# Moving products and weighings from VectorE to GpSimd, and a scaling to ScalarE, in a four-layer kernel on one core

## The chip, the core and the metric

The kernel runs on one core of a Trainium2 chip. Its engines are TensorE (PE in the profile, its weight loads PEld), VectorE (DVE), ScalarE (ACT), GpSimd (POOL) and SyncE (SP), which only issues DMAs here. The metric is the device time of one execution in microseconds; lower is better.

## What is computed

One sequence of 1024 tokens of width 256 passes through four blocks, each followed by a layer norm of the input plus the block's output:

```python
x = layernorm(x + selective_scan_block(x))   # layer 0: 32 states, 256 channels
x = layernorm(x + quantized_ffn(x))          # 704 hidden
x = layernorm(x + mamba_block(x))            # layer 1: conv, 16 states, 512 channels, gate
x = layernorm(x + attention_and_experts(x))  # 16 heads of 128; 16 experts, 6 a token, and a shared one
```

Both scans have the same core, for each channel d and state n:

```python
delta = softplus(projection + bias)
h[t] = exp(delta[t] * A[d, n]) * h[t-1] + (delta[t] * u[t]) * B[t, n]
y[t] = sum_n h[t] * C[t, n]
```

In layer 0 u is the input itself, in layer 1 the convolved and activated input. The attention is causal, behind a root-mean-square norm (`x * rsqrt(mean(x^2) + eps) * w`); a second such norm stands ahead of the experts, where each expert's hidden value `silu(g) * up` is multiplied by the token's weight for this expert and projected down.

## The kernel before

The tokens are taken in four chunks of 256 (c = 0 to 3). A scan unit is one state n of a pair of channel tiles (2 x 128 channels by 256 tokens); each layer has 32 units a chunk, 256 units in all. For a unit:
- SP fetches the state's B and C rows, broadcast to all partitions (`bc_rows`, five buffers, L1303).
- ScalarE makes the decays exp(delta * A), two instructions, into a PSUM bank (L1700).
- GpSimd makes the drive: `w` times the B row (L2291), w being delta times u.
- VectorE scans, two instructions of 128x256 (L1957), and multiplies the states by the C row (L1969; in chunk 0 GpSimd does so for a quarter of the units, L2301).
- ScalarE copies the last states into `h_end` for the next chunk (L1713).
- In chunk 0 TensorE adds the units up in PSUM (L1410), in the others GpSimd does (L2321).

Between the scans of layer 0 and layer 1 of a chunk lies a chain of small steps (norms, the quantized FFN, the convolution, projections, softplus). Softplus ends in `softplus_sum` on VectorE: four elementwise instructions on 128x512, then delta (L2020), then w, by L2028 in layer 0 and by L2024 in layer 1, where the factor 0.5 is part of it. There are three softplus calls a chunk (layer 0, and two halves of layer 1), so 12 in all. `x_proj` (L1483) makes the time step and the B and C rows of layer 1 from the weight `w_x1`, which ScalarE halves once (`chore`, L1682).

Behind layer 1 a chunk goes through the attention, 16 heads one after the other, which VectorE and ScalarE share (maxima L2144, exponentials L1865, moves L2160 and L1876). Ahead of the heads (r = 0) and ahead of the experts (r = 1) stands the root-mean-square norm: ScalarE squares with a row sum (L1813), VectorE takes the mean (L2129), GpSimd the power -1/2 (L2324), VectorE scales the tokens into `hn` (`rms_scale`, L2135, two instructions), TensorE turns them (L1394), ScalarE moves them into `hT` (L1826).

The experts run in 13 groups of up to two tiles: 2 shared and 11 routed. For a group TensorE makes gate and up (L1388), ScalarE a tanh (L1907), VectorE two products (L2240, L2248) and for the 11 routed groups the weighing by `cw_rows`, the routing weights of 128x512 (`weigh_up`, L2259); TensorE projects down (L1652). Four `hh` buffers hold the groups.

The order of instructions on each engine is not written by hand. A planner (`weave`, L738) holds lanes of stages; each stage has parts with an engine and an assumed cost, events it comes after, events it gives, and a lag behind its end. Again and again it takes, over all lanes, the part with the smallest key:

```python
start = max(ready, clock[engine])
key = (start - lane.bonus * EARLIER[engine], -lane.bonus, ready)
```

and emits it, if it belongs to the engine being written. So the costs and each lane's bonus set the order in every queue, the DMA queue of SP included. Twelve weight loads (L1289) have a lane of their own: load i comes after scan i + 1.

Of the kernel before, what the change touches and what calls it, by code (L numbers as in the profile page):

```python
# [17 lines left out]
P = 128  # L18
# [30 lines left out]
AOTS, HIDDENS = 3, 4  # L49

# [46 lines left out]
def blocks(c):  # L97

    return SIZES[c] // P
# [64 lines left out]
class Idle:  # L164
# [7 lines left out]
    load = load_x = dbc = project_dt = softplus_abs = softplus_x = softplus_log = softplus_sum = chore = nothing  # L172
# [55 lines left out]
DMA = "sp", 0.3  # L228
# [34 lines left out]
class Units:  # L263
# [20 lines left out]
    def fetches(self):  # L284
        total = CHUNKS * sum(UNITS)
        while len(self.order) < total:
# [12 lines left out]
            yield Stage(partial(self.p.fetch, g, c, layer, k), (DMA,), after, (("rows", g),), lag=3.0)  # L299
# [23 lines left out]
    def drives(self):  # L323
        for unit in self.each():
# [4 lines left out]
            after = [("delta", c, 0 if layer == 0 else 1 + k // STATE1), ("rows", g)]  # L329
# [78 lines left out]
class Chain:  # L408
# [6 lines left out]
    def lanes(self):  # L415
        return [Lane(self.first(), 0.20, 8), Lane(self.second(), 1.30, 16)]

    def softplus(self, c, g, given, use):
# [8 lines left out]
        before = (("decays", b, layer), ("drives", b, layer)) if b >= 0 else ()  # L427
        yield Stage(partial(p.softplus_sum, c, g), (dve(size, *[2 * size] * 5),),
                    (("log", c, g), ("x", c, g), *before), (("delta", c, g), ("scratch", "softplus", c, g)))

    def first(self):
        p = self.p
        for c in range(CHUNKS):
            size = SIZES[c]
            yield Stage(partial(p.load_x, c), (DMA,), (("y", c - 2, 0),) if c > 1 else (), (("x0", c),), lag=4.0)
# [70 lines left out]
    def second(self):  # L506
        for c in range(CHUNKS):
# [6 lines left out]
         "ident_b", "w_o")  # L514
FFN_LOADS, MAMBA_LOADS = 3, 7
# [14 lines left out]
class Attention:  # L530
# [5 lines left out]
    def lanes(self):  # L536
        return [Lane(self.into_heads(), 0.60, 8), Lane(self.projections(), 0.60, 8), Lane(self.scores(), 1.00, 6),
                Lane(self.products(), 1.10, 8), Lane(self.results(), 1.10, 8), Lane(self.experts(), 2.50, 2),
                Lane(self.routing(), 1.50, 8), Lane(self.weights(), 2.20, 2),
                Lane(self.hidden(), 1.20, 6),  # L540
                Lane(self.weighed(), 1.90, 4), Lane(self.sums(), 1.80, 6)]

    def rms(self, c, r, given):
# [7 lines left out]
        yield Stage(partial(p.rms_scale, c, r), (dve(*[DIM + 150] * n),), (("rms", c, r),), (("scaled", c, r),))  # L551
# [3 lines left out]
    def into_heads(self):  # L555

        p = self.p
        for c in range(CHUNKS):
            for h in range(HEADS):
# [6 lines left out]
                yield Stage(partial(p.fetch_head, c, h), (DMA,), after, (("head_w", c, h),), lag=4.0)  # L566
                if c:
                    yield Stage(partial(p.place, c, h), (DMA,), self.kv_free(c, h), (("past", c, h),), lag=4.0)

# [86 lines left out]
    def experts(self):  # L656

        p = self.p
        for c in range(CHUNKS):
            for n in range(len(FETCHES)):  # L660
# [9 lines left out]
                yield Stage(partial(p.fetch_expert, c, n), (DMA,), after, (("expert", c, n),), lag=4.5)  # L670
# [15 lines left out]
    def weights(self):  # L686

        p = self.p
        for c in range(CHUNKS):
            for r, rows in enumerate(CW_ROWS):  # L690
                bc, br = divmod(c * ROUTED_GROUPS + r - CW, ROUTED_GROUPS)
                free = (("weighted", bc, SHARED_GROUPS + br),) if bc >= 0 else ()
                yield Stage(partial(p.fetch_weights, c, r), (("sp", 0.1 * len(rows)),), (("cwT", c), *free),
                            (("cw", c, r),), lag=4.0)
# [13 lines left out]
    def weighed(self):  # L708
        p = self.p
        for c in range(CHUNKS):  # L710
            for g in range(SHARED_GROUPS, N_GROUPS):
                width = len(GROUPS[g]) * SIZES[c]
                yield Stage(partial(p.weigh_up, c, g), (dve(width),),
                            (("cw", c, g - SHARED_GROUPS), ("raised", c, g)), (("weighted", c, g),))

    def sums(self):
        p = self.p
        for c in range(CHUNKS):
# [8 lines left out]
            yield Stage(partial(p.store, c), (DMA,), (("out", c),), (("hn", c, 2),), lag=4.0)  # L727

EARLIER = {'pe': 0.2, 'dve': 0.2, 'act': 0.7, 'pool': 1.0, 'sp': 1.0}


LOADED = {("first",): 5.5}
# [1708 lines left out]
```

## Time and profile before

| | |
|---|---|
| median of 3 runs | 1362.71 us (1359.16 to 1363.14) |
| profiled execution | 1363.67 us, of which the span of instructions is 1362.4 |
| mean granted TensorE clock | 0.922 |
| busy: TensorE, its weight loads | 1119.7 us (82%), 879.8 us (65%) |
| busy: VectorE, ScalarE, GpSimd | 1030.9 us (76%), 596.2 us (44%), 600.4 us (44%) |
| DMA | 191.54 MB, mean 141 GB/s |

Shares are of the span. The durations below come from the one profiled execution. A line number can be that of a helper: L1388 is every projection on TensorE.

### The profile page before, as it was taken

To read this page: it belongs to the slowest core of one execution; us is meant where nothing else is said; L and a number is where in the kernel's file an instruction comes from. 1 tells how busy PE (TensorE), PEld (TensorE's weight loads), DVE (VectorE), ACT (ScalarE), POOL (GpSimd) and SP (SyncE) were. 2 spreads that over 40 slices of the span, in tenths; PEclk is the share of its full clock that TensorE was granted. 3 is DMA by queue.
4 is the path that set the end of the run, shared out by engine and by line. 5 is a ranking of instruction groups with operands and counts; after the bars stand their busy time and mean duration, and the time that the engine had idled before them with its cause. 6 is when DMAs were issued, how large, how long until landed. Compare 5 with 4: busy or idle time off the path is not lost. (4 is left out here: it accounts for less than half of the span.)

```text
span 1362.4 us, 17002 instructions
## 1 busy us (share of the span) xinstructions
PE 1119.7 (82%) x5224; PEld 879.8 (65%) x5224; DVE 1030.9 (76%) x1879; ACT 596.2 (44%) x1543; POOL 600.4 (44%) x487
## 2 busy tenths in 40 slices
PE   4557536499695899977977899799998999999797
PEld 2335324377584678755855787587877877777586
DVE  5797899989999999999997885699944444444433
ACT  4553555454664336555753232565532123333210
POOL 3577477964575687654875640176600000000000
PEclk9798758899797999998988999899999999999899
DMA  4652124353254775433765641266543643222173
GB/s 135 251 195 74 48 88 142 108 158 105 85 174 155 218 232 166 136 101 111 210 216 156 196 144 43 83 201 199 162 144 104 204 136 104 95 93 81 58 210 103
DMA packets 105434, 191.54 MB, mean 141 GB/s; under 512 B 11648, under 2 KB 42368, under 8 KB 105088
## 3 DMA queue, kind: packets, MB, share of 16 engines
q1 hardware_dynamic: 91520, 177.42, 41.9%
q10 hardware_dynamic: 13824, 13.05, 3.1%
q8 instruction: 41, 0.67, 0.2%
q14 instruction: 49, 0.40, 0.1%
HBM read 176.33 MB, written 14.09 MB: 140 GB/s over the span
## 5 line engine op out<-in xcount | busy, mean ns | idle before, releaser
L1957 DVE TENSOR_TENSOR_SCAN scan_banks<-scan_banks,h_end,drive 128x256 f32<-128x256 f32 x480 | 338.5, 742 | 13.9 <-POOL drive L2291 11.0
L2321 POOL TENSOR_TENSOR sum<-sum,state 128x512 f32<-128x512 f32 x174 | 227.3, 1306 | 54.4 <-DVE state L1969 52.3
L2291 POOL TENSOR_TENSOR drive<-w0T,bc_rows 128x512 f32<-128x512 f32 x128 | 164.3, 1291 | 152.0 <-DVE scan_banks L1957 98.0
L2291 POOL TENSOR_TENSOR drive<-w1T,bc_rows 128x512 f32<-128x512 f32 x128 | 163.4, 1283 | 139.6 <-DVE scan_banks L1957 61.4
L2324 POOL TENSOR_TENSOR stats_b<-stats_b,neg_half 128x2 f32<-128x2 f32 x12 | 8.8, 732 | 367.4 <-DVE stats_b L2129 200.8
L1969 DVE TENSOR_TENSOR state<-scan_banks,bc_rows 128x512 f32<-128x512 f32 x240 | 162.7, 678 | 0.6
L1410 PE MATMUL score_banks<-state,ident 128*128 128x256 f32 x256 | 85.2, 483 | 79.3 <-DVE state L1969 44.7
L1560 PE MATMUL score_banks<-kv,qT 128*128 128x512 f32 (+3 forms) x360 | 135.7, 493 | 6.4 <-ACT probs L1865 3.7
L2144 DVE TENSOR_REDUCE soft<-score_banks 128x1 f32<-128x128 f32 (+4 forms) x122 | 88.0, 729 | 61.9 <-PE score_banks L1562 61.6
L1865 ACT ACTIVATE probs<-score_banks,soft 128x128 f32<-128x128 f32 (+4 forms) x122 | 87.8, 721 | 97.5 <-DVE soft L2144 96.7
L1410 PEld LDWEIGHTS score_banks<-state,ident 128*128 128x128 f32 x256 | 57.2, 239 | 107.5 <-DVE state L1969 57.4
L1585 PE MATMUL work_bank<-probsT,kv 128*128 128x256 f32 x504 | 120.6, 363 | 5.3 <-DVE pad_hs L2107 2.7
L1388 PE MATMUL work_bank<-hT,streamed_w 128*128 128x256 f32 x496 | 122.0, 388 | 1.5 <-ACT kv L1834 1.4
L1700 ACT ACTIVATE scan_banks<-delta1T,a 128x256 f32<-128x256 f32 x256 | 111.4, 470 | 24.6 <-DVE state L1969 17.1
L1700 ACT ACTIVATE scan_banks<-delta0T,a 128x256 f32<-128x256 f32 x256 | 110.9, 468 | 25.3 <-DVE state L1969 22.0
L1388 PEld LDWEIGHTS work_bank<-hT,streamed_w 128*128 128x128 f32 x496 | 92.3, 195 | 14.2 <-ACT kv L1834 2.2
L1585 PEld LDWEIGHTS work_bank<-probsT,kv 128*128 128x128 f32 x504 | 87.9, 193 | 15.2 <-DVE probsT L2160 3.6
L1713 ACT ACTIVATE h_end<-scan_banks 128x2 f32<-128x2 f32 x176 | 29.7, 171 | 154.5 <-DVE state L1969 138.4
L1560 PEld LDWEIGHTS score_banks<-kv,qT 128*128 128x128 f32 x360 | 63.4, 194 | 42.4 <-issue 33.8
L1394 PE MATMUL work_bank<-ident,probs 128*128 128x128 f32 x450 | 72.7, 280 | 16.8 <-DVE pad_hs L2107 7.5
L2160 DVE COPY probsT<-work_bank 128x512 f32<-128x512 f32 (+2 forms) x132 | 58.6, 471 | 23.5 <-PE work_bank L1394 22.9
L1394 PEld LDWEIGHTS work_bank<-ident,probs 128*128 128x128 f32 x450 | 53.2, 144 | 35.8 <-issue 9.8
(203 smaller groups left out, 2098.6 us busy)
## 6 DMA issues: line engine op xcount, KB each, us to landing
bc_rows<-bc_rows SPq DMA_DIRECT2D x256, 256.0 KB, 3.8
streamed_w<-in_w_head SPq DMA_DIRECT2D x64, 384.0 KB, 5.0
expert_w<-in_w_moe SPq DMA_DIRECT2D x52, 384.0 KB, 4.4
kv_past<-kv ACTq DMA_DIRECT2D x48, 256.0 KB, 3.2
kv<-in_w_moe SPq DMA_DIRECT2D x32, 384.0 KB, 3.9
kv<-kv_past SPq DMA_DIRECT2D x16, 768.0 KB, 4.7
kv<-kv_past SPq DMA_DIRECT2D x16, 512.0 KB, 5.0
streamed_w<-in_w_moe SPq DMA_DIRECT2D x16, 384.0 KB, 4.1
```

The source lines that it names most:

```text
L1388: instruction = self.matmul(to, weight, m, start=k == 0, stop=k == len(weights) - 1)
L1394: instruction = self.transpose(b[:, at:at + P], src, ident[:, :])
L1410: done = self.matmul(to[:, i, :], ident[:, :], tiles[:, i, :], start=n == 0 and i == 0, stop=n == STATES[layer] - 1, skip_group_check=True)
L1560: self.matmul(to[:, at:upto], q[h % 2][:, qb * P:(qb + 1) * P], tile[:, 0, at:upto], start=True, stop=upto < n_keys)
L1585: mm = self.matmul(b[:, lo:hi], tile[:, 1, kb * HEAD:(kb + 1) * HEAD], moving[:, i * hi + lo:(i + 1) * hi], start=kb == 0, stop=kb == last ...
L1700: done = self.activation(to[:, i * size:(i + 1) * size], delta_of(layer, c)[:, kt, 0:size], ACT.Exp, scale=a_rate[layer][:, kt, n:n + 1])
L1865: self.activation(probs[probs_at(c, h, qb)][:, 0:n_keys], b[:, 0:n_keys], ACT.Exp, bias=st[:, 0, qb:qb + 1], accum_out=st[:, 1, qb:qb + 1] ...
L1957: done = e.engine.tensor_tensor_scan(states, decays, drive[g % len(drive)][:, i, 0:size], h_end[layer][:, n, kt:kt + 1], ALU.mult, ALU.add)
L1969: self.tt(slot_of(c, layer, k), by_tile(unit_bank(g, size), size), rows_of(g, c, 1), ALU.mult).then_inc(weighed, 1)
L2144: e.engine.tensor_reduce(st[:, 0, qb:qb + 1], b[:, 0:keys(c, qb)], AX.X, ALU.max, negate=True).then_inc(neg_max, 1)
L2291: self.tt(drive[g % len(drive)][:, :, 0:size], w_of(layer, c)[:, PAIR * half:PAIR * (half + 1), 0:size], rows_of(g, c, 0), ALU.mult).then_ ...
L2321: self.tt(to, so_far, slot_of(c, layer, k), ALU.add).then_inc(added, 1)
```

## The change

- **Products.** `softplus_sum` on VectorE ends with delta. A new stage `delta_x` on GpSimd multiplies delta by the input (x0 or hs) into w. The factor 0.5 of layer 1 goes into the B columns of `w_x1`: the one ScalarE instruction on this weight becomes three, with 0.5, 0.25 and 0.5. delta's last add waits for the previous product that used the buffer, not for the drives; the drives are waited for by `delta_x`.
- **Scaling.** `rms_scale` moves from VectorE to ScalarE, a Copy with a scale for each token.
- **Weighing.** `weigh_up` of chunks 0 and 1 moves from VectorE to GpSimd; chunks 2 and 3 stay.
- **Loads.** Load i comes after scan 2i + 1.
- **Planner.** New costs for matmuls, turns and DMAs (these now by size, as time of the SP queue), new lags, and a new bonus for 20 lanes and new factors on it by engine (`EARLIER`).

```diff
+WEIGHED_BY_POOL = 2
 def pe(*columns):
-    return "pe", sum(0.018 + 0.00172 * n for n in columns)
+    return "pe", sum(0.012 + 0.00169 * n for n in columns)
 def pe_turn(n):
-    return "pe", 0.13 * n
+    return "pe", 0.115 * n
-DMA = "sp", 0.3
+def dma(kilobytes):
+    return "sp", max(0.5, kilobytes / 230)
...
-        return [Lane(self.fetches(), 0.00, 1), Lane(self.decays(), 0.60), Lane(self.drives(), 0.30), Lane(self.scans(), 0.10),
-                Lane(self.weighs(), 1.05), Lane(self.carries(), 0.90), Lane(self.adds(), 0.40), Lane(self.skips(), 0.90)]
+        return [Lane(self.fetches(), 2.30, 1), Lane(self.decays(), 0.70), Lane(self.drives(), 0.10), Lane(self.scans(), -0.60),
+                Lane(self.weighs(), 0.75), Lane(self.carries(), 2.40), Lane(self.adds(), 0.20), Lane(self.skips(), -0.40)]
...
-            after = [("delta", c, 0 if layer == 0 else 1 + k // STATE1), ("rows", g)]
+            after = [("w", c, 0 if layer == 0 else 1 + k // STATE1), ("rows", g)]
...
-        return [Lane(self.first(), 0.20, 8), Lane(self.second(), 1.30, 16)]
+        return [Lane(self.first(), 0.50, 8), Lane(self.second(), 1.30, 16)]
...
-        before = (("decays", b, layer), ("drives", b, layer)) if b >= 0 else ()
-        yield Stage(partial(p.softplus_sum, c, g), (dve(size, *[2 * size] * 5),),
+        before = (("decays", b, layer), ("w", b, g)) if b >= 0 else ()
+        yield Stage(partial(p.softplus_sum, c, g), (dve(size, *[2 * size] * 4),),
                     (("log", c, g), ("x", c, g), *before), (("delta", c, g), ("scratch", "softplus", c, g)))
+        before = (("drives", b, layer),) if b >= 0 else ()
+        yield Stage(partial(p.delta_x, c, g), (pool(2 * size),), (("delta", c, g), *before), (("w", c, g),))
...
-        yield Stage(partial(p.load, i), (DMA,), (("scan", i + 1),), (("in", i),), lag=10.0)
+        yield Stage(partial(p.load, i), (dma(LOADED_KB[i]),), (("scan", 2 * i + 1),), (("in", i),), lag=4.0)
...
-        return [Lane(self.into_heads(), 0.60, 8), Lane(self.projections(), 0.60, 8), Lane(self.scores(), 1.00, 6),
-                Lane(self.products(), 1.10, 8), Lane(self.results(), 1.10, 8), Lane(self.experts(), 2.50, 2),
-                Lane(self.routing(), 1.50, 8), Lane(self.weights(), 2.20, 2),
-                Lane(self.hidden(), 1.20, 6),
-                Lane(self.weighed(), 1.90, 4), Lane(self.sums(), 1.80, 6)]
+        return [Lane(self.into_heads(), 0.90, 8), Lane(self.projections(), 0.60, 8), Lane(self.scores(), 1.30, 6),
+                Lane(self.products(), 0.90, 8), Lane(self.results(), 1.90, 8), Lane(self.experts(), 2.20, 2),
+                Lane(self.routing(), 1.60, 8), Lane(self.weights(), 1.50, 2),
+                Lane(self.hidden(), 1.60, 6),
+                Lane(self.weighed(), 2.40, 4), Lane(self.sums(), 2.30, 6)]
...
-        yield Stage(partial(p.rms_scale, c, r), (dve(*[DIM + 150] * n),), (("rms", c, r),), (("scaled", c, r),))
+        yield Stage(partial(p.rms_scale, c, r), (act(*[DIM] * n),), (("rms", c, r),), (("scaled", c, r),))
...
-                yield Stage(partial(p.weigh_up, c, g), (dve(width),),
+                yield Stage(partial(p.weigh_up, c, g), (pool(width) if c < WEIGHED_BY_POOL else dve(width),),
...
-EARLIER = {'pe': 0.2, 'dve': 0.2, 'act': 0.7, 'pool': 1.0, 'sp': 1.0}
+EARLIER = {'pe': 0.3, 'dve': 0.1, 'act': 0.7, 'pool': 1.0, 'sp': 1.0}
...
-    lanes = [*Chain(p).lanes(), Lane(load_lane(p), 1.0), Lane(chore_lane(p), -0.10), *units.lanes(), *Attention(p).lanes()]
+    lanes = [*Chain(p).lanes(), Lane(load_lane(p), 1.0), Lane(chore_lane(p), -0.90), *units.lanes(), *Attention(p).lanes()]
...
-                wait_unit(e, driven, c - 1 if layer else c - 2, layer)
+                e.wait_ge(w_ready[layer], c - 1 if layer else c - 2, half)
                 self.tt(to, cs, ls, ALU.add).then_inc(delta_ready[layer].sem, 1)
-                e.wait_ge(delta_ready[layer], c, half)
-                if layer:
-                    e.wait_ge(hs_ready, c)
-                    self.stt(to_w, hs[:, 2 * half:2 * half + 2, 0:size], 0.5, to, ALU.mult,
-                             ALU.mult).then_inc(w_ready[1].sem, 1)
-                else:
-                    e.wait_ge(x0_in[c % 2], c // 2)
-                    self.tt(to_w, to, x0s[c % 2][:, :, 0:size], ALU.mult).then_inc(w_ready[0].sem, 1)
...
+            def delta_x(self, c, g):
+
+                e, size, layer, half = self.e, SIZES[c], min(g, 1), max(g - 1, 0)
+                of, to = (t(layer, c)[:, 2 * half:2 * half + 2, 0:size] for t in (delta_of, w_of))
+                e.wait_ge(delta_ready[layer], c, half)
+                wait_unit(e, driven, c - 1 if layer else c - 2, layer)
+                if layer:
+                    e.wait_ge(hs_ready, c)
+                    x = hs[:, 2 * half:2 * half + 2, 0:size]
+                else:
+                    e.wait_ge(x0_in[c % 2], c // 2)
+                    x = x0s[c % 2][:, :, 0:size]
+                self.tt(to, of, x, ALU.mult).then_inc(w_ready[layer].sem, 1)
```

## Rows read from the trace of the kernel before

**Rows 1.** The page's first part: busy us, share of the span, instructions of each engine.

```profile
PE 1119.7 (82%) x5224; PEld 879.8 (65%) x5224; DVE 1030.9 (76%) x1879; ACT 596.2 (44%) x1543; POOL 600.4 (44%) x487
```

**Rows 2.** Busy time by stretch (instructions), then granted clock, DMA share, GB/s.

```profile
core 0: us, PE busy (x) PEld busy (x) DVE busy (x) ACT busy (x) POOL busy (x), PEclk, DMA share, GB/s
0.00:290.00 290.00, 160.62 (x532) 111.81 (x533) 243.75 (x416) 145.05 (x377) 188.88 (x156) 0.81 0.42 134
290.00:985.00 695.00, 604.12 (x2947) 484.26 (x2946) 622.18 (x1157) 354.60 (x957) 404.39 (x323) 0.94 0.50 154
985.00:1362.00 377.00, 354.93 (x1749) 283.75 (x1747) 164.92 (x308) 96.56 (x211) 7.15 (x9) 0.98 0.39 122
```

**Rows 3.** Waits of TensorE, 290 to 985 us: us in total, times, longest.

```profile
PE work_bank L1394 <- DVE hn L2135: 18.0, 3, 11.4
PE work_bank L1652 <- DVE hh L2259: 15.4, 13, 3.7
...
PE work_bank L1388 <- DVE hsT L2114: 0.3, 1, 0.3
```

**Rows 4.** Groups by line: count | busy us, mean ns | idle before them.

```profile
L2259 DVE TENSOR_TENSOR hh<-hh,cw_rows 128x512 f32<-128x512 f32 x44 | 34.6, 787 | 1.8 <-DMA cw_rows<-cw 1.0
...
L2135 DVE TENSOR_SCALAR hn<-x,stats_b 128x256 f32<-128x256 f32 x16 | 11.7, 772 | 0.8 <-POOL stats_b L2324 0.8
...
L2024 DVE SCALAR_TENSOR_TENSOR w1T<-hsT,delta1T 128x512 f32<-128x512 f32 x8 | 5.5, 691 | 0.3
...
L2028 DVE TENSOR_TENSOR w0T<-delta0T,x0T 128x512 f32<-128x512 f32 x4 | 3.7, 928 | 0.1
```

**Rows 5.** The weighings (L2259) alone, by stretch.

```profile
290.00:985.00 695.00, 19.40 (x22) 0.94 0.50 154
```

**Rows 6.** The scalings (L2135) alone, by stretch.

```profile
0.00:290.00 290.00, 2.04 (x2) 0.81 0.42 134
290.00:985.00 695.00, 6.85 (x8) 0.94 0.50 154
985.00:1362.00 377.00, 2.82 (x6) 0.98 0.39 122
```

**Rows 7.** The products of layer 1 (L2024) alone, by stretch.

```profile
290.00:985.00 695.00, 4.15 (x6) 0.94 0.50 154
```

**Rows 8.** The products of layer 0 (L2028) alone, by stretch.

```profile
290.00:985.00 695.00, 0.69 (x1) 0.94 0.50 154
```

**Rows 9.** Timelines of VectorE and of GpSimd around 468 us: start, us.

```profile
468.13 1.70 DVE L2259 TENSOR_TENSOR hh<-hh,cw_rows 128x512 f32<-128x512 f32 x1
...
466.77 2.50 POOL L2291 TENSOR_TENSOR drive<-w1T,bc_rows 128x512 f32<-128x512 f32 x2
469.23 3.14 POOL L2321 TENSOR_TENSOR sum<-sum,state 128x512 f32<-128x512 f32 x2
```

**Rows 10.** Groups by line, for the prices on GpSimd and ScalarE.

```profile
L1813 ACT ACTIVATE hn<-x 128x256 f32<-128x256 f32 x16 | 6.5, 407 | 9.2 <-DVE x L2174 6.1 <-DVE x L2042 3.1
...
L2339 POOL TENSOR_TENSOR x<-x 128x512 f32<-128x512 f32 x4 | 5.1, 1275 | 0.0
```

**Rows 11.** Busy time in the stretches of chunk 0's and chunk 1's experts.

```profile
445.00:515.00 70.00, 62.55 (x276) 51.99 (x276) 65.73 (x104) 26.54 (x74) 53.52 (x41) 0.98 0.71 223
735.00:815.00 80.00, 71.67 (x319) 59.41 (x318) 64.84 (x112) 23.94 (x59) 49.15 (x39) 0.94 0.61 187
```

**Rows 12.** Waits of GpSimd, 0 to 120 us.

```profile
POOL drive L2291 <- DMA bc_rows<-bc_rows: 24.3, 11, 4.4
POOL drive L2291 <- DVE w0T L2028: 17.6, 1, 17.6
```

**Rows 13.** The scans as a group: the last column is VectorE's idle time.

```profile
L1957 DVE TENSOR_TENSOR_SCAN scan_banks<-scan_banks,h_end,drive 128x256 f32<-128x256 f32 x480 | 338.5, 742 | 13.9 <-POOL drive L2291 11.0 <-ACT scan_banks L1700 1.6 <-issue 1.4
```

**Rows 14.** Timeline of VectorE, the last scan.

```profile
982.73 0.75 DVE L1957 TENSOR_TENSOR_SCAN scan_banks<-scan_banks,h_end,drive 128x256 f32<-128x256 f32 x1
```

More of the change, by code:

```diff
@@ L170, in nothing @@
         pass
-    load = load_x = dbc = project_dt = softplus_abs = softplus_x = softplus_log = softplus_sum = chore = nothing
+    load = load_x = dbc = project_dt = softplus_abs = softplus_x = softplus_log = softplus_sum = delta_x = chore = nothing
     fetch = decay = drive = scan = weigh = carry = add_up = skip0 = skip1 = nothing
@@ L298, in fetches @@
             after = ((f"rows{layer}", c),) + ((("weigh", g - ROWS),) if g >= ROWS else ())
-            yield Stage(partial(self.p.fetch, g, c, layer, k), (DMA,), after, (("rows", g),), lag=3.0)
+            yield Stage(partial(self.p.fetch, g, c, layer, k), (dma(SIZES[c]),), after, (("rows", g),), lag=2.4)
     def each(self):
@@ L434, in first @@
             size = SIZES[c]
-            yield Stage(partial(p.load_x, c), (DMA,), (("y", c - 2, 0),) if c > 1 else (), (("x0", c),), lag=4.0)
+            yield Stage(partial(p.load_x, c), (dma(size),), (("y", c - 2, 0),) if c > 1 else (), (("x0", c),), lag=2.4)
             yield Stage(partial(p.dbc, c), (pe(size, size), act(size)), (("x0", c), ("first",)),
@@ L514 @@
          "ident_b", "w_o")
+LOADED_KB = (704, 704, 768, 1024, 320, 256, 512, 16, 128, 32, 32, 2048)
 FFN_LOADS, MAMBA_LOADS = 3, 7
@@ L669, in experts @@
                     after = (("qk_mm", c, HEADS - 4 + LENT), ("v_mm", c, HEADS - 4 + LENT))
-                yield Stage(partial(p.fetch_expert, c, n), (DMA,), after, (("expert", c, n),), lag=4.5)
+                yield Stage(partial(p.fetch_expert, c, n), (dma(3 * DIM * P / 256),), after, (("expert", c, n),), lag=2.4)
     def routing(self):
@@ L692, in weights @@
                 free = (("weighted", bc, SHARED_GROUPS + br),) if bc >= 0 else ()
-                yield Stage(partial(p.fetch_weights, c, r), (("sp", 0.1 * len(rows)),), (("cwT", c), *free),
-                            (("cw", c, r),), lag=4.0)
+                yield Stage(partial(p.fetch_weights, c, r), (("sp", 0.45 * len(rows)),), (("cwT", c), *free),
+                            (("cw", c, r),), lag=2.4)
     def hidden(self):
@@ L1681, in chore @@
                     e.wait_value(mamba_in, MAMBA_IN)
-                    self.activation(w_x1[:, :, :], w_x1[:, :, :], ACT.Copy, scale=0.5).then_inc(adjusted.sem, 1)
+                    for lo, hi, scale in ((0, P, 0.5), (P, P + STATE1, 0.25), (P + STATE1, P + 2 * STATE1, 0.5)):
+                        columns_ = w_x1[:, :, lo:hi]
+                        self.activation(columns_, columns_, ACT.Copy, scale=scale).then_inc(adjusted.sem, 1)
             def decay(self, g, c, layer, k):
@@ L1814, in rms_square, with rms_scale @@
                 done.then_inc(squared[r].sem, 1)
+            def rms_scale(self, c, r):
+                e, st, x, n = self.e, stats_b[r], (x3[c % 2], x4)[r], blocks(c)
+                e.wait_ge(rms_ready[r], c)
+                for tb in range(n):
+                    done = self.activation(hn[:, tb, :], x[:, tb, :], ACT.Copy, scale=st[:, tb, 2:3])
+                done.then_inc(rms_scaled[r].sem, 1)
             def rms_turn(self, c, r):
@@ L2004, in softplus_sum @@
                 cs = by_tile(s[:, 0:KD * size], size)
-                to, to_w = (t(layer, c)[:, 2 * half:2 * half + 2, 0:size] for t in (delta_of, w_of))
+                to = delta_of(layer, c)[:, 2 * half:2 * half + 2, 0:size]
                 e.wait_ge(sp_exp[layer], c, half)
@@ L2129, in rms_mean @@
                 self.ts(st[:, 0:n, 1], st[:, 0:n, 0], 1.0 / DIM, RMS_EPS, ALU.mult, ALU.add).then_inc(mean_sq[r].sem, 1)
-            def rms_scale(self, c, r):
-                e, st, x, n = self.e, stats_b[r], (x3[c % 2], x4)[r], blocks(c)
-                e.wait_ge(rms_ready[r], c)
-                for tb in range(n):
-                    done = self.ts(hn[:, tb, :], x[:, tb, :], st[:, tb, 2:3], None, ALU.mult)
-                done.then_inc(rms_scaled[r].sem, 1)
             def score(self, c, h, qb):
@@ L2333, in rms_mean, with weigh_up @@
                 self.to_power(stats_b[r], 2, 1, blocks(c)).then_inc(rms_ready[r].sem, 1)
+            def weigh_up(self, c, g):
+                if g < SHARED_GROUPS or c >= WEIGHED_BY_POOL:
+                    return
+                e, upto = self.e, len(GROUPS[g]) * SIZES[c]
+                to = hh[g % len(hh)][:, 0:upto]
+                e.wait_ge(moe_up, c, g)
+                r = g - SHARED_GROUPS
+                e.wait_value(cw_in[cw_at(c, r)], 16 * cw_loads(c, r))
+                size = SIZES[c]
+                self.tt(by_tile(to, size), by_tile(to, size), cw_rows[cw_at(c, r)][:, 0:len(GROUPS[g]), 0:size],
+                        ALU.mult).then_inc(moe_weighed.sem, 1)
             def residual(self, c):
```

12 lines of the change are left out of this document (6 added, 6 removed).

## The prediction

> **What bounds the kernel now.** I read the page's busy shares first. They show two engines near their limit in turn, TensorE with 1119.7 us and VectorE with 1030.9 us of a 1362.4 us span, and two with room, GpSimd among them at 44% [rows 1]. An average hides which one sets the end, so the second view is the busy time by stretch. Up to 290 us (chunk 0's two scans and the chain between them) VectorE has 243.75 of 290 us and TensorE only 160.62. From 290 to 985 us, while scans of chunks 1 to 3 run beside the attention and experts of chunks 0 to 2, VectorE has 622.18 and TensorE 604.12 of 695 us: both near full. After 985 us GpSimd is nearly empty, so the scans are over, and TensorE has 354.93 of 377 us: pure TensorE work [rows 2]. The third view is what TensorE waited for between 290 and 985 us. It was idle 695 - 604.12 = 90.9 us there, and the 12 rows released by VectorE make 72.9 us of that, from the scaled rows hn (18.0) down to 0.3 us [rows 3].
>
> So the end is: what VectorE takes to open the attention (290 us), then TensorE's work plus the gaps that VectorE's late results leave in it. A microsecond taken off VectorE counts in full before 290 us, partly from 290 to 985 us, and hardly after.
>
> **What leaves VectorE.** Three things: the products delta times x (12), the scaling by the root mean square (16), and of the 44 weighings of expert values the 22 of chunks 0 and 1 [rows 4]. By stretch:
> - Weighings: all 22 of chunks 0 and 1 lie in 290 to 985 us and took 19.40 us [rows 5].
> - Scalings: 2.04 us before 290, 6.85 up to 985, 2.82 behind [rows 6].
> - Products: 5.5 + 3.7 us in all [rows 4], of which 4.15 + 0.69 lie in 290 to 985 us [rows 7, 8], so 4.4 before.
>
> Before 290 us that is 4.4 + 2.0 = 6.4 us, in the middle 19.4 + 6.9 + 4.8 = 31.1 us.
>
> These durations carry a surcharge that leaves as well. One weighing took 1.70 us, where a product of the same shape takes 0.69 [rows 4]: it began at 468.13, when GpSimd was at work until 469.27, and ended some 0.6 us after that; GpSimd's next two adds then took 3.14 us together [rows 9]. The sums above are of measured durations, so they hold it already.
>
> **What arrives elsewhere.**
> - GpSimd gets 12 products and 22 weighings of 128x512. The nearest row is its undisturbed add of the same shape, 1.275 us [rows 10]: 34 x 1.275 = 43.4 us on an engine with 404.39 of 695 us busy in the middle [rows 2], where 7 products and 22 weighings fall (37 us, to some 441). On average there is room. In the experts' stretches there is less: 53.52 of 70 us and 49.15 of 80 us are busy [rows 11]; with 11 weighings (14.0 us) each they come to 67.5 and 63.2 us. The first is nearly full.
> - ScalarE gets 16 scalings of 128x256. Nearest row, a Square of that shape from SBUF: 0.407 us [rows 10], so 6.5 us, with 354.60 of 695 us busy [rows 2]: hidden, and each pair (0.8 us) is no longer than VectorE's 1.5 us (11.7/16 x 2) [rows 4]. At the last chunk's routing, where the chain is bare, that gives about 0.7 us back.
> - One wait is new: the first drive of a chunk needs the product from GpSimd (1.28 us) instead of VectorE (0.69) [rows 4, 10], 0.6 us more. It is bare where GpSimd stood waiting for the product, as for 17.6 us at the start [rows 12]. Two such places before 290 us (one per layer): +1.2. At the later ones TensorE has other work. Behind a late product stand all drives and adds in GpSimd's own queue, and VectorE's scans wait for those.
> - delta's last add now waits for the previous product instead of the previous chunk's last drive; it still waits for the last decay, which reads the same buffer, so nothing is won: 0.
> - The two extra ScalarE instructions on w_x run once, before 290 us, where ScalarE has 145.05 of 290 us [rows 2]: hidden, 0.
>
> **The loads.** Twelve weight loads are issued behind scans 1, 3, ... 23 instead of 1 to 12, on SP's queue, between the fetches of the B and C rows. Up to 120 us GpSimd waited 24.3 us for those rows [rows 12], but VectorE's scans waited only 11.0 us for drives in the whole span [rows 13]. So the gain lies between 0 and 11 us; a loss would need the last load (w_o) to come after the first attention at 290 us, and the 256 scan units end at 983.5 us [rows 14], 3.8 us each, so that unit 23 is over by some 92 us: excluded. I take 2 us, nearer to zero, because the fetches also compete with each other.
>
> **The order.** The planner's costs, lags and precedence change, so all five queues are reordered. No row prices that. Bounds: it can at best take the rest of TensorE's idle time behind 290 us (90.9 + 22.1 = 113 us [rows 2]), and nothing bounds what it loses but the same gaps doubled. Chains of dependent steps make most of these gaps, so I carry a third either way (37 us) into the outer rivals and take 0.
>
> **The sum.** Before 290 us: -6.4 - 2 + 1.2 = -7.2. In the middle: were VectorE the only bound, the stretch would shrink by its load, 695 x 31.1/622.18 = 34.7 us; were TensorE the only bound, by 0. Both are near full (90% and 87%), so I take the half: -17.4. At the end -0.7. Together -25.3. The profiled execution took 1363.67 us (1362.4 of span and 1.3 around it), so 1338.4; it lies 1 us above the median of the runs, 1362.71. I predict **1338 us**.
>
> A rule that speaks against this change stands in the Trainium skill (GPSIMD Engine Reference, Engine selection): elementwise work belongs on VectorE, GpSimd being about twice as slow with two inputs. The trace agrees, with 1.275 against 0.69 us [rows 4, 10]. By that rule alone, with the receiving engine as the bound, the middle would grow by the 37 us put on GpSimd, to 1363.7 - 7.9 + 37 = 1393 us. The 441 of 695 us above speak against it for the middle as a whole; for single stretches it is taken up below.
>
> **Rivals.**
> - VectorE alone bounds the middle: the full 34.7 us comes, and with -7.9 outside it -42.6: 1321 us. For it: four fifths of TensorE's idle time there ends on VectorE [rows 3]. Against: with the stretch at 660 us TensorE would have to be busy 604/660 = 91.5% beside scans. Reordering may carry it down to 1300. Chance 0.20.
> - GpSimd takes over in the experts' stretches (67.5 of 70 us): the 19.4 us of weighings bring nothing, half of the other 11.7 us remains (5.9), with 7.9 outside: -13.8, 1350 us, with reordering 1340 to 1362. Chance 0.14.
> - Slower: the weighing stands in GpSimd's queue behind a drive and an add (2.5 us) and takes 0.6 us longer, and TensorE's down-projection waits for it. 22 groups x 3.1 us = 68 us if all of it is bare. It decides once over 25 of these 68 us come through, or if the new order leaves gaps of that size; at 60% bare it gives 1338 + 41 = 1379 us. For it: TensorE already waited 15.4 us for weighed values [rows 3]. Against: four hh buffers let three groups run ahead. Chance 0.16.
> - My forecast, half of the load comes through: 1338, own range 1324 to 1352. Chance 0.50.
>
> **Chances and range.** A measurement can tell about 0.3% (4 us) from no change. Faster by more: 0.50 + 0.20 + 0.08 of the third = 0.78. Within: 0.06 of the third and 0.01 of the slower one = 0.07. Slower: 0.15. The range leaves out a tenth at either side: below, half of the first rival (under 1306); above, the slower two thirds of the slower one, over 1368.
>
> **What would show it.** VectorE's busy time near 1031 - 19.4 - 11.7 - 9.2 = 991 us; GpSimd's near 644; the last scan over at some 959 us instead of 983 [rows 14]; TensorE's wait for hn below 18 us, for the weighed hh not above 15. Wrong is the forecast if GpSimd is busy over 95% of the experts' stretch of chunk 0 and TensorE's wait on its weighing grows to tens of microseconds, or if scans end early and TensorE's idle time behind 290 us stays at 113 us.

## The result

| | before | after |
|---|---|---|
| median of 4 runs each | 1361.43 us | 1345.14 us |
| profiled execution (span) | 1363.67 (1362.4) | 1343.95 (1342.6) |
| mean granted TensorE clock | 0.922 | 0.928 |

The ratio of after to before is 0.9886 (95% interval 0.9864 to 0.9909): 16.3 us faster, where 25 were forecast. The direction and the range held; the size did not. The two profiled executions lie 19.7 us apart, since that of before was slower than its four timed runs and that of after as fast as its fastest, so some 3 us of the differences between traces below are scatter.

The first part of the page of after, engine by engine:

```profile
span 1342.6 us, 17016 instructions
...
PE 1120.5 (83%) x5224; PEld 879.7 (66%) x5224; DVE 994.4 (74%) x1829; ACT 605.5 (45%) x1561; POOL 635.8 (47%) x521
```

Against [rows 1] TensorE's work is unchanged, VectorE lost 36.5 us and GpSimd gained 35.4. So the load moved as it was meant to, and the span's 19.8 us can only be time in which TensorE used to be idle: 242.7 us of it before, 222.1 after.

Fixed stretches would compare different pieces of work, so I cut both traces at two events: the first ScalarE move into hT, which opens chunk 0's attention, and the last scan. Busy time by stretch between these cuts, first of before, then of after (columns as in [rows 2]):

```profile
0.00:271.10 271.10, 143.95 (x448) 97.94 (x448) 228.06 (x385) 134.90 (x342) 175.66 (x146) 0.80 0.40 130
271.10:983.50 712.40, 619.28 (x3020) 496.81 (x3021) 637.08 (x1187) 363.72 (x988) 416.90 (x333) 0.94 0.50 155
983.50:1362.40 378.90, 356.43 (x1758) 285.07 (x1756) 165.71 (x309) 97.59 (x214) 7.87 (x9) 0.98 0.39 121
```

```profile
0.00:260.90 260.90, 143.14 (x448) 97.82 (x448) 224.67 (x382) 136.94 (x351) 184.85 (x153) 0.80 0.44 136
260.90:973.10 712.20, 625.35 (x3050) 501.40 (x3051) 609.49 (x1151) 371.20 (x999) 443.05 (x360) 0.94 0.51 156
973.10:1342.60 369.50, 352.02 (x1728) 280.51 (x1726) 160.23 (x298) 97.32 (x212) 7.88 (x9) 0.99 0.39 122
```

Read the first number behind each stretch. The opening is 10.2 us shorter. From there to the last scan nothing is won, 712.4 against 712.2 us, although VectorE does 27.6 us less in it. Behind the last scan 9.4 us are won. In the middle TensorE did 6.1 us more work in the same time and was idle 86.9 us instead of 93.1; behind the scans it then had 4.4 us less left to do and 5.0 us less idle time. So the scans end sooner only by what the opening won; the relief of VectorE does not show in the length of the middle. The experiments below show why: in the traces the new order costs there what the moves gain.

TensorE's waits for the moved results over the whole span of after (total, times, longest):

```profile
PE work_bank L1404 <- ACT hn L1832: 22.8, 4, 7.5
PE work_bank L1662 <- POOL hh L2362: 14.6, 12, 2.9
...
PE work_bank L1662 <- DVE hh L2263: 4.9, 3, 2.9
```

In before they were 32.6 us for hn and 17.8 for hh over the whole span. The 17.8 are of all 44 weighings, and so compare with 14.6 + 4.9 = 19.5 us in after; the 22 of chunks 0 and 1 alone had 15.4 [rows 3] and have 14.6. So TensorE waits less for hn, but hardly less for the weighings that moved. The moved instructions on GpSimd, and its own adds:

```profile
L2362 POOL TENSOR_TENSOR hh<-hh,cw_rows 128x512 f32<-128x512 f32 x22 | 27.9, 1268 | 20.9 <-DVE hh L2252 14.8 <-DMA cw_rows<-cw 6.2
...
L2339 POOL TENSOR_TENSOR sum<-sum,state 128x512 f32<-128x512 f32 x174 | 221.5, 1273 | 67.1 <-DVE state L1988 64.3
```

### The profile page after: what moved, and what is told of

Same layout as the page of the kernel before. It is cut to its first block and busy times, and to the rows that moved or that the text cites. A ratio compares the mean times of both kernels' runs of the same rounds, so it can differ in the third digit from the quotient of the medians.

```text
span 1342.6 us, 17016 instructions
## 1 busy us (share of the span) xinstructions
PE 1120.5 (83%) x5224; PEld 879.7 (66%) x5224; DVE 994.4 (74%) x1829; ACT 605.5 (45%) x1561; POOL 635.8 (47%) x521
## 5 line engine op out<-in xcount | busy, mean ns | idle before, releaser
L1976 DVE TENSOR_TENSOR_SCAN scan_banks<-scan_banks,h_end,drive 128x256 f32<-128x256 f32 x480 | 337.2, 743 | 16.3 <-POOL drive L2295 13.3
L2339 POOL TENSOR_TENSOR sum<-sum,state 128x512 f32<-128x512 f32 x174 | 221.5, 1273 | 67.1 <-DVE state L1988 64.3
L1398 PE MATMUL work_bank<-hT,streamed_w 128*128 128x256 f32 x548 | 134.4, 387 | 3.5 <-DVE x L2178 3.1
L1595 PE MATMUL work_bank<-probsT,kv 128*128 128x256 f32 (+1 forms) x532 | 129.0, 366 | 6.8 <-ACT probsT L1895 4.7
L1398 PEld LDWEIGHTS work_bank<-hT,streamed_w 128*128 128x128 f32 x548 | 103.2, 194 | 18.3 <-DVE x L2178 4.2
L1570 PE MATMUL score_banks<-kv,qT 128*128 128x512 f32 (+3 forms) x316 | 113.1, 473 | 1.7 <-ACT kv L1865 1.7
L1884 ACT ACTIVATE probs<-score_banks,soft 128x128 f32<-128x128 f32 (+3 forms) x111 | 76.0, 685 | 77.2 <-DVE soft L2148 76.8
L2148 DVE TENSOR_REDUCE soft<-score_banks 128x1 f32<-128x128 f32 (+3 forms) x111 | 75.1, 682 | 41.4 <-PE score_banks L1572 40.5
L1595 PEld LDWEIGHTS work_bank<-probsT,kv 128*128 128x128 f32 x532 | 93.3, 195 | 18.5 <-ACT probsT L1895 5.1
L1570 PEld LDWEIGHTS score_banks<-kv,qT 128*128 128x128 f32 x316 | 53.5, 190 | 30.1 <-issue 25.3
L2164 DVE COPY probsT<-work_bank 128x256 f32<-128x256 f32 (+2 forms) x125 | 54.7, 465 | 20.6 <-PE work_bank L1404 19.1
```

The costliest lines, as they stand in the source:

```text
L1398: instruction = self.matmul(to, weight, m, start=k == 0, stop=k == len(weights) - 1)
L1570: self.matmul(to[:, at:upto], q[h % 2][:, qb * P:(qb + 1) * P], tile[:, 0, at:upto], start=True, stop=upto < n_keys)
L1595: mm = self.matmul(b[:, lo:hi], tile[:, 1, kb * HEAD:(kb + 1) * HEAD], moving[:, i * hi + lo:(i + 1) * hi], start=kb == 0, stop=kb == last ...
L1884: self.activation(probs[probs_at(c, h, qb)][:, 0:n_keys], b[:, 0:n_keys], ACT.Exp, bias=st[:, 0, qb:qb + 1], accum_out=st[:, 1, qb:qb + 1] ...
L1976: done = e.engine.tensor_tensor_scan(states, decays, drive[g % len(drive)][:, i, 0:size], h_end[layer][:, n, kt:kt + 1], ALU.mult, ALU.add)
L2148: e.engine.tensor_reduce(st[:, 0, qb:qb + 1], b[:, 0:keys(c, qb)], AX.X, ALU.max, negate=True).then_inc(neg_max, 1)
```

## The experiments

Two theories stood. **A, the moves:** what gains is the load taken off VectorE, and the new planner numbers only follow it. **B, the order:** the gain comes from the new order of the queues, and the moves are worth little alone. A third came up in between. **C, the fit:** the time of such a kernel depends on details of the order by more than the moves are worth, and each kernel is as fast as it is because its numbers are fitted to its own instructions.

### Each half of the change alone, re-planned

**moves_old_plan**: after, with before's costs, lags, bonuses and load times. For example:

```diff
-                Lane(self.weighed(), 2.40, 4), Lane(self.sums(), 2.30, 6)]
+                Lane(self.weighed(), 1.90, 4), Lane(self.sums(), 1.80, 6)]
...
-        yield Stage(partial(p.load, i), (dma(LOADED_KB[i]),), (("scan", 2 * i + 1),), (("in", i),), lag=4.0)
+        yield Stage(partial(p.load, i), (dma(LOADED_KB[i]),), (("scan", i + 1),), (("in", i),), lag=10.0)
```

> The changed kernel with the planner's numbers of before (costs, lags, bonuses, factors) and the loads behind scans 1 to 12: only the three moves of work are left. Theory A, the moves bring the gain (40 us taken from VectorE): 1338 to 1350 us, 12 us or more under the kernel before. Rival B, the new order brings it: within 4 us of the kernel before, or slower. VectorE's busy time near 995 us under both.

**plan_only**: after, with products, scaling and weighing back on VectorE:

```diff
-WEIGHED_BY_POOL = 2
+WEIGHED_BY_POOL = 0
...
-        yield Stage(partial(p.delta_x, c, g), (pool(2 * size),), (("delta", c, g), *before), (("w", c, g),))
+        yield Stage(partial(p.delta_x, c, g), (dve(2 * size),), (("delta", c, g), *before), (("w", c, g),))
...
-        yield Stage(partial(p.rms_scale, c, r), (act(*[DIM] * n),), (("rms", c, r),), (("scaled", c, r),))
+        yield Stage(partial(p.rms_scale, c, r), (dve(*[DIM + 150] * n),), (("rms", c, r),), (("scaled", c, r),))
```

> The changed kernel with products, scalings and weighings back on VectorE; all new planner numbers and the spread loads stay. Theory A: 1357 to 1368 us, as the kernel before. Rival B: 1345 to 1350 us, most of the gain. VectorE's busy time near 1031 us.

**no_weigh**: only `WEIGHED_BY_POOL = 0`.

> The changed kernel with the weighings of chunks 0 and 1 back on VectorE (WEIGHED_BY_POOL = 0). If half of their 19.4 us came through: 1355 us. If GpSimd is the limit in the experts' stretches and they brought nothing: 1345 us or less. If they are the whole of the gain behind 290 us: 1358 us or more.

**loads_early**: only the loads' event back to `("scan", i + 1)`.

> The changed kernel with load i behind scan i + 1 again. The attention of the changed kernel opened 10.2 us earlier (hT of chunk 0 at 260.9 instead of 271.1 us), 3 us more than the sum said. If the loads are the reason: 1347 to 1349 us, hT of chunk 0 near 264 to 266 us. If they are nothing: 1344 to 1346 us and hT at 261 us.

| kernel | median us | ratio to before (95%) |
|---|---|---|
| moves_old_plan | 1368.29 | 1.0067 (1.0046 to 1.0088) |
| plan_only | 1372.14 | 1.0096 (1.0078 to 1.0114) |
| no_weigh | 1368.04 | 1.0063 (1.0045 to 1.0081) |
| loads_early | 1347.79 | 0.9895 (0.9875 to 0.9915) |

Either half alone is slower than before. Theory A in its plain form falls: moves_old_plan has the whole relief of VectorE and loses 0.7%. So does B: the new plan without the moves loses 1.0%. no_weigh came out slower than every expectation for it: putting 22 weighings back and planning again costs 23 us, more than the whole gain. The busy times of moves_old_plan:

```profile
PE 1116.9 (82%) x5224; PEld 879.2 (64%) x5224; DVE 992.8 (73%) x1829; ACT 604.5 (44%) x1561; POOL 634.7 (47%) x521
```

They are those of after within 4 us on each engine, at a span 21 us longer: busy time says nothing of this difference. The loads' new times are worth nothing that shows: the median of loads_early lies in the range expected if the loads mattered, but its interval overlaps that of after, and its attention opens at 261.8 us, where that expectation had 264 to 266. In loads_early GpSimd's wait for rows up to 120 us is 11.5 us and in after 12.6, against 24.3 in before [rows 12], so other parts of the change halved that wait.

But these four have a flaw: each move changes the planner's clocks, so every queue is reordered again, and a comparison mixes the move with a new order.

### The same moves in a held order

In the next kernels the planner runs with the costs and engines of the parent, so that the order of all queues stays its own, and only when a part is emitted is it given to the other engine. TensorE's and SyncE's queues are identical to the parent's (the traces show the same 5224 instructions and the same 636 DMAs in the same order); a moved instruction takes the place in its new queue that the planned order gives. An entry of ELSEWHERE names the planned engine, the engine that takes the work over, and the stage.

```diff
-        if p.engine == engine:
+        if p.engine == engine or (engine, p.engine, stage.run.func.__name__) in ELSEWHERE:
```

**before_order_moved**: before's order, all three moves made. **after_order_unmoved**: after's order, all three moves undone. Beside them, **before_nudged** and **after_nudged** change one number by 0.05, the bonus of the decays' lane: 0.60 to 0.65 in before, 0.70 to 0.75 in after.

> The order of every queue as in the kernel before (TensorE's and SP's instruction lists are the same); only the products, the scalings and the 22 weighings are issued on GpSimd and ScalarE, each at the place in the plan where VectorE had it. Theory A, the moves gain by themselves and the re-planned variant lost it to a worse order: 1336 to 1350 us. Rival B, a move gains only with an order that fits it: 1357 us or more. VectorE busy near 991 us.

> The order of the changed kernel held, the three kinds of work back on VectorE, each at its place in the plan. Theory A: 15 to 30 us slower than the changed kernel (1360 to 1375 us), since VectorE has 36 us more to do. Rival B, the order is the gain: 1345 to 1352 us.

> The kernel before with one number of the planner changed, the bonus of the decays 0.65 instead of 0.60, which reorders some queues but moves no work. Theory C, both kernels' planner numbers fit their own set of work and any other order costs some 5 to 15 us: 1366 to 1376 us. Rival: orders near by are all alike, 1358 to 1365 us.

> The changed kernel with the bonus of the decays 0.75 instead of 0.70. Theory C: 1350 to 1360 us, part or all of the gain gone. Rival: 1342 to 1349 us.

| kernel | median us | ratio to before (95%) |
|---|---|---|
| before_order_moved | 1372.62 | 1.0092 (1.0075 to 1.0109) |
| after_order_unmoved | 1373.28 | 1.0088 (1.0069 to 1.0107) |
| before_nudged | 1398.66 | 1.0281 (1.0262 to 1.0300) |
| after_nudged | 1370.91 | 1.0074 (1.0054 to 1.0095) |

What the moves do in after's order shows in TensorE's waits of after_order_unmoved (whole span; after has 22.8 us for hn, and 19.5 for the hh of all 44 weighings):

```profile
PE work_bank L1407 <- DVE hn L2156: 27.2, 4, 8.2
PE work_bank L1665 <- DVE hh L2280: 24.9, 16, 3.2
```

In the stretches between opening and last scan the same kernel has:

```profile
0.00:268.00 268.00, 146.77 (x448) 100.74 (x448) 229.21 (x389) 135.67 (x350) 178.56 (x148) 0.78 0.42 133
268.00:1003.80 735.80, 631.65 (x3050) 506.20 (x3051) 638.98 (x1187) 366.81 (x991) 408.56 (x331) 0.93 0.49 151
1003.80:1376.00 372.20, 353.52 (x1728) 281.74 (x1726) 164.03 (x305) 94.56 (x206) 7.88 (x9) 0.98 0.39 121
```

So from before to this kernel the order (with the loads and the split of `w_x1`, which stay) takes the opening from 271.1 to 268.0 us, the middle from 712.4 to 735.8 and the end from 378.9 to 372.2; from here to after the moves take 7.1, 23.6 and 2.7 us off. (This profiled execution was 4 us above the kernel's median.)

What the nudge does to before shows in the stretches of [rows 2] (the last one is longer, as the span is 1396.1 us):

```profile
0.00:290.00 290.00, 161.96 (x541) 112.68 (x542) 244.21 (x420) 147.36 (x384) 188.44 (x156) 0.82 0.40 135
290.00:985.00 695.00, 582.09 (x2811) 466.14 (x2812) 610.24 (x1130) 344.69 (x927) 399.92 (x321) 0.92 0.48 150
985.00:1396.00 411.00, 383.34 (x1875) 306.23 (x1874) 177.99 (x331) 106.37 (x233) 10.00 (x11) 0.97 0.37 117
```

The opening is as before; in the middle TensorE gets 22 us less work done (582.09 against 604.12), all of which is left for the end. TensorE's own busy time also grew over the span, from 1119.7 to 1127.4 us, at a granted clock of 0.92 instead of 0.94 in the middle. And the nudge is small as a number but not as an order: 2662 of TensorE's 5224 instructions stand at the same place in its queue as in before.

Two things follow. First, after_order_unmoved fell where theory A had it and before_order_moved where rival B had it: the same moves cost 12 us in one order and gain 28 us in the other (1.0088 against 0.9886). Their worth is no number of its own. Second, a nudge that moves no work costs 38 us in before (1398.66 against 1360.56 of before beside it) and 25.8 us in after (1370.91 against 1345.14). That is the direction of C, and in both kernels more than C expected (1366 to 1376 and 1350 to 1360 us): after_nudged is slower than before. One nudge for each is a small sample; it shows the size of the effect, not its distribution.

### Where the moves hurt before's order

TensorE's waits over the whole span of before_order_moved:

```profile
PE work_bank L1405 <- ACT hn L1833: 30.5, 5, 10.2
PE work_bank L1663 <- POOL hh L2366: 29.1, 15, 9.0
...
PE work_bank L1663 <- DVE hh L2264: 2.1, 2, 1.6
```

The wait for hn is like before's (32.6); that for the weighed values is up from 17.8 to 29.1 + 2.1 = 31.2 us. The timelines of VectorE, GpSimd and TensorE around one of its long ones show how (start, us; in brackets the idle time before and what ended it):

```profile
448.40 0.67 DVE L2253 SCALAR_TENSOR_TENSOR hh<-work_bank,hh 128x512 f32<-128x512 f32 x1
...
451.29 1.26 POOL L2296 TENSOR_TENSOR drive<-w1T,bc_rows 128x512 f32<-128x512 f32 x1 [5.19 <-DMA bc_rows<-bc_rows]
452.51 1.26 POOL L2343 TENSOR_TENSOR sum<-sum,state 128x512 f32<-128x512 f32 x1
453.73 1.27 POOL L2296 TENSOR_TENSOR drive<-w1T,bc_rows 128x512 f32<-128x512 f32 x1
454.95 1.26 POOL L2366 TENSOR_TENSOR hh<-hh,cw_rows 128x512 f32<-128x512 f32 x1
...
456.27 2.07 PE L1663 MATMUL work_bank<-streamed_w,hh 128*128 128x256 f32 x4 [6.72 <-POOL hh L2366]
```

The value to be weighed is ready at 449.07. GpSimd stands idle then, but at a drive whose B and C rows have not landed; behind it in the queue come an add and another drive, and only then the weighing, 5.9 us late. TensorE waits 6.7 us. At chunk 1's experts the same happens: ready at 731.02, a drive waits 7.57 us for its rows, the weighing starts at 739.17, 8.2 us late, TensorE waits 9.0 us. GpSimd was idle 16 of the 84 us of that first stretch:

```profile
440.00:524.00 84.00, 70.98 (x313) 59.20 (x312) 63.35 (x103) 31.16 (x87) 67.93 (x55) 0.95 0.62 196
```

So it is not full (67.93 of 84 us, 81%); the weighing stands in the wrong place. At chunk 1 what blocks it is an old wait. Waits of GpSimd for rows in chunk 1's experts' stretch, first before's (723 to 811 us), then before_order_moved's (721 to 818 us):

```profile
POOL drive L2291 <- DMA bc_rows<-bc_rows: 11.3, 6, 7.5
```

```profile
POOL drive L2296 <- DMA bc_rows<-bc_rows: 13.2, 6, 7.6
```

In before no weighing stands in GpSimd's queue, so no down-projection stands behind these 11.3 us; with the weighings there, it does. With only the weighings left on VectorE (before_order_two_moved, below) GpSimd still waits 12.5 us for rows at chunk 1, and TensorE's longest wait for a weighed value is 3.5 us. At chunk 0 the 5.19 us above are a new wait: in before GpSimd's longest for rows there is 1.5 us, and why it grew was not looked into. In after GpSimd does not wait for rows at all in that stretch, and 0.7 us in chunk 0's. Its plan gives the fetches a bonus of 2.30 in place of 0.00. That this number alone removes the wait wasn't tried.

### One move at a time in a held order

Before's order with products and scalings moved but not the weighings (**before_order_two_moved**: before_order_moved with `WEIGHED_BY_POOL = 0`); after's order with one move undone each. ELSEWHERE holds one entry each; for the weighings `WEIGHED_BY_POOL` also becomes 0, while the planner keeps their cost on GpSimd:

```diff
+ELSEWHERE = {('pool', 'dve', 'weigh_up')}      # after_order_weigh_back
+ELSEWHERE = {('pool', 'dve', 'delta_x')}       # after_order_delta_back
+ELSEWHERE = {('act', 'dve', 'rms_scale')}      # after_order_scale_back
```

> The order of before held, products and scalings moved, all weighings left on VectorE. With the weighings moved too the same order took 1372.6 us, 12 us more than the kernel before. Theory D, the weighings behind GpSimd's drives and adds are that loss: 1350 to 1359 us, under the kernel before. Rival, any shift against the planned order costs: 1363 us or more.

> The changed kernel's order held, the 22 weighings of chunks 0 and 1 back on VectorE in place, products and scalings stay moved. All three back cost 28 us (1373.3 against 1345.1). Theory A, VectorE's load decides in this order, so the cost goes by the load given back (19.4 of 40 us): 1356 to 1362 us. Rival B, weighing on GpSimd costs time in this order too, as it seems to in the order of before (its experts' stretches are 6 and 9 us longer there): 1345 us or less.

> The changed kernel's order held, only the 12 products back on VectorE. Theory A (by load, 9 of 40 us): 1350 to 1354 us, a part of it before the attention opens (hT of chunk 0 near 264 to 266 us instead of 261). Rival: nothing outside the noise, 1343 to 1348 us.

> The changed kernel's order held, only the 16 scalings by the root mean square back on VectorE. Theory A (by load, 12 of 40 us, and a chain that TensorE waits for): 1351 to 1356 us. Rival: nothing, 1343 to 1348 us.

| kernel | ratio to before (95%) | the move's worth |
|---|---|---|
| before_order_two_moved | 0.9966 (0.9951 to 0.9982) | products and scalings -0.34%; the weighings then +1.26% |
| after_order_weigh_back | 0.9964 (0.9952 to 0.9976) | weighings -0.78% (10.6 us) |
| after_order_delta_back | 0.9959 (0.9939 to 0.9978) | products -0.73% (9.9 us) |
| after_order_scale_back | 0.9987 (0.9973 to 1.0000) | scalings -1.01% (13.7 us) |

(The worth is the difference of two ratios, times 1361 us; after's own is 0.9886, measured at another time and the same in all three, so each of these three carries some 0.3%, 4 us, of uncertainty.)

In before's order the weighings turn a gain of 4.6 us into a loss of 12.5: 17 us for this one move, and the term that decides the sign. before_order_two_moved lies in the range of theory D. Its stretches between opening and last scan, then those of before_order_moved:

```profile
0.00:269.20 269.20, 141.97 (x448) 97.67 (x448) 222.96 (x379) 135.84 (x347) 179.83 (x150) 0.81 0.41 132
269.20:971.60 702.40, 615.43 (x3020) 494.66 (x3021) 621.07 (x1170) 367.15 (x996) 425.92 (x341) 0.94 0.51 157
971.60:1350.30 378.70, 359.25 (x1758) 287.36 (x1756) 163.35 (x304) 100.23 (x220) 7.87 (x9) 0.98 0.39 121
```

```profile
0.00:270.80 270.80, 143.59 (x448) 98.31 (x448) 222.12 (x379) 135.82 (x347) 180.04 (x150) 0.80 0.39 131
270.80:990.20 719.40, 620.97 (x3020) 498.10 (x3021) 606.28 (x1148) 367.06 (x996) 445.75 (x363) 0.94 0.49 153
990.20:1369.40 379.20, 357.75 (x1758) 286.36 (x1756) 163.14 (x304) 100.26 (x220) 7.88 (x9) 0.98 0.39 121
```

The middle, 712.4 us in before, is 702.4 with products and scalings moved and 719.4 with the weighings moved too: 10.0 us won, then 17.0 lost. (The first execution lies 4 us under the kernel's median, so part of the 10.0 may be scatter.) TensorE's waits of before_order_two_moved beside before_order_moved's above:

```profile
PE work_bank L1405 <- ACT hn L1833: 31.2, 5, 10.2
PE work_bank L1663 <- DVE hh L2264: 17.1, 15, 3.5
```

The wait for hh is back at 17.1 us from 31.2. That is 14.1 of the 17 us; of the other 3 the runs tell nothing.

In after's order all three moves gain, 34 us one by one and 28 together, which is within the uncertainty, and not in proportion to the work: the weighings had 19.4 us on VectorE, the scalings 11.7, the products 9.2. After theory A, by load, only after_order_weigh_back (1356.27 us) came out in its range; after_order_delta_back (1355.29) and after_order_scale_back (1359.87) cost more than theirs. In after_order_scale_back TensorE's waits are

```profile
PE work_bank L1407 <- DVE hn L2142: 26.7, 4, 8.0
PE work_bank L1665 <- POOL hh L2365: 17.3, 11, 3.0
```

against 22.8 and 14.6 in after: 6.6 us of its 13.7 (with 4 us of uncertainty) lie in these two.

## Why the prediction was right in direction and wrong in size

Two terms failed. The order was put at 0: in the traces it costs 13.6 us (after_order_unmoved against before: 23.4 lost in the middle, 9.8 won outside it; by the ratios 12.0 in all). The middle was put at half of VectorE's relief, -17.4: the moves gave -23.6 there in after's order and +7.0 in before's, where the weighings' place in GpSimd's queue, which the sum put at nothing, cost 17.0. That the total fell near the forecast owes much to luck, since the moves' larger gain and the order's cost offset each other; so does the direction, where a nudge of 0.05 costs more than the whole gain. Point by point:

- **Loads of the engines: right.** VectorE 994 us (forecast 991), GpSimd 636 (644), its weighings 1.268 us each (1.275). A pair of scalings on ScalarE took 0.91 us instead of the 0.8 taken (497 ns each in the median, the second beginning before the first is over), a tenth of a microsecond.
- **Before 290 us: -10.2 instead of -7.2.** The first attention opens at 260.9 us instead of 271.1. With after's plan and none of the moves (plan_only) it opens at 263.7, with before's plan and all moves at 267.1; in after's held order without the moves at 268.0. In before's held order with the moves it opens at 270.8. So the moves give 0 to 7 us by the order they meet, forecast 5.2, and the plan the rest. The loads' -2 did not show: loads_early opens at 261.8.
- **The middle: 0 instead of -17.4.** The last scan starts at 972.32 instead of 982.73 [rows 14], all of it from the opening; forecast was an end at 959. In a held order of after the last scan does come 31 us later without the moves (1003.08), of which 7 us in the opening. Relief of VectorE does shorten the middle, there even by more than the forecast. In before's order the last scan comes 6.8 us later with the moves (989.48), but not because relief is worth nothing: products and scalings, 11.7 us of load there, took 10.0 us off the middle, and the weighings put 17.0 back. The half was not a bound between two engines; what comes through depends on the order and on the place that the work takes in its new queue: 23.6 of 34.7 us in one order, -7.0 in the other.
- **Behind the scans: -9.4 instead of -0.7.** The forecast took this stretch as fixed TensorE work. It is not: TensorE took 4.4 us of it into the middle, and 5.0 us of its gaps closed. 6.7 of the 9.4 us are there in after_order_unmoved already, so they belong to the order.
- **The order: not 0.** I put a third of 113 us (37) either way on it and then left it out of the sum. The runs show 25.8 and 38 us from a nudge of 0.05, so the size in the range was right.
- **The rivals.** VectorE alone as the bound (1321) did not come. GpSimd taking over in the experts' stretches (1350) is nearest in time but not in mechanism. Forecast were 67.5 of 70 us busy; in chunk 0's stretch of after there are 70.61 of 84:

```profile
432.00:516.00 84.00, 73.50 (x321) 61.21 (x322) 68.06 (x108) 33.98 (x94) 70.61 (x58) 0.96 0.71 206
```

  That is 84%. The slower rival, the weighing behind drives and adds in GpSimd's queue, is real: it is what before_order_moved shows. Its place was right, its price was not: not 3.1 us at each of 22 groups, but 6 to 8 us at the first routed group of a chunk, where a drive ahead of it waits for a DMA. In after it does not decide; TensorE's wait for the weighed values of chunks 0 and 1 is 14.6 us, below the 15 that I gave as the sign, though it was only 15.4 before. The wait for hn in the middle is 11.5 us, below the 18. The other sign of being wrong did not come either: behind 290 us TensorE is idle 102.5 us instead of 113.

**What stays open.** Which features of an order make it 26 or 38 us better than its neighbour. One is named, fetches late in front of a queued weighing (14 us at TensorE), but before_nudged has its weighings on VectorE and loses 38 us without it. The granted clock is a rival that no run separates. In no_weigh the same 5224 TensorE instructions are busy for 1137.6 us at a mean clock of 0.919, in after for 1120.5 at 0.928: 17.1 of the 26.0 us between the two traces; in after_order_unmoved it is 11.4 of 33.4. Executions of one kernel scatter the same way, before between 1354.90 us at 0.932 and 1369.18 at 0.918. Whether gaps in an order lower the clock, or the clock adds its own part, is not shown. No version beat after: loads_early equals it within the intervals.

## What to carry to other kernels

Where a planner writes the queues, a move of work and a new order are two experiments. Test the move with the order held (give the instruction to the other engine only at emission), and test the order by nudging a number that should not matter; where a nudge is worth 2%, no gain of 1% from one re-plan can be put down to the move. Before an instruction goes to an engine with room, look at what waits stand in that engine's queue ahead of the place it will take: idle time that costs nothing today is paid by whatever is queued behind it tomorrow.

## What the runs showed of the hardware

VectorE and GpSimd slow each other down. The 22 weighings of chunks 0 and 1 on VectorE in before, then the 22 of chunks 2 and 3, where GpSimd has almost nothing to do (shortest, median and longest in ns):

```profile
L2259 DVE TENSOR_TENSOR hh<-hh,cw_rows x22: 681/692/1696, 454.9 to 807.8; 128x512 f32<-128x512 f32 x22
...
L2259 DVE TENSOR_TENSOR hh<-hh,cw_rows x22: 691/691/693, 1043.8 to 1353.9; 128x512 f32<-128x512 f32 x22
```

Nine of the first 22 took over 0.75 us, and each of the nine began while GpSimd was at work. The one of 1.70 us ended 0.6 us after the drive at its start, with GpSimd's next add under way [rows 9]. The 16 scalings, one input of 128x256, show it too: 340 to 1374 ns, and the eight over 0.75 us all began beside GpSimd. The 34 weighings and products that left took 28.6 us on VectorE [rows 4, 5]; at the 0.69 us of an undisturbed one they would be 23.5.

GpSimd's add of states took 1273 ns in the mean in after against 1306 in before. The held orders show what the weighings have to do with it. In before's order their move alone takes the mean from 1299 to 1271 ns; in after's order there is nothing of the kind, 1275 ns with all three moves undone. So which of the two engines pays depends on the order as well.

The Trainium skill (GPSIMD Engine Reference, Key points) says that the two engines share their interfaces to SBUF, and that a VectorE instruction with two SBUF inputs contends with GpSimd; the 1.70 us agree with it, and in before's order the shorter adds do too.

The Trainium skill's advice against such moves (GPSIMD Engine Reference, Engine selection), twice the time on GpSimd with two inputs, nearly agrees in the price, 1.268 against 0.69 us. As a verdict it holds in one order and not in the other: in before's order the weighings' move lost 17 us, in after's order the weighings and the products gained some 10 us each, with VectorE 86% busy from the opening to the last scan.
